# Expert stage of a mixture-of-experts kernel: expert numbers read once in eight steps, table places eight at a time, stores issued from other queues

## The reference

```
x = x + rwkv_block(layernorm(x))     # time mix: projections, a scan over 1024 tokens; channel mix
x = x + ffn(layernorm(x))
# ffn, over N = 8192 tokens:
gates = sigmoid(xt @ expert_sel.T)                 # 32 experts
sel_val, sel_idx = top_k(gates, 4)                 # 4 experts per token
scores = relu(einsum('nd,edf->nef', xt, keys))     # keys:   32 x 256 x 128
out = einsum('nef,efv->nv', scores * gate_full, values)   # values: 32 x 128 x 256
```

## Time and profile before

| | us |
|---|---|
| median of three runs | 1266.48 |
| the profiled execution's own time | 1261.35 |
| its span, first to last instruction | 1259.5 |
| PE / PEld busy | 1107.5 (88%) / 953.2 (76%) |
| DVE / ACT / POOL busy | 1015.1 (81%) / 752.8 (60%) / 760.8 (60%) |
| mean granted TensorE clock | 0.958 |

### The profile page before, as it was taken

One profiled execution on the slowest core, in us unless ns is written; L12 is line 12 of the kernel. 1 busy time (PEld: TensorE's weight loads), 2 busy tenths in 40 slices (PEclk: granted clock), 3 DMA queues, 4 the chain that ended last, 5 costly groups with the idle time before them and its releaser, 6 DMA issues.

```text
span 1259.5 us, 24103 instructions
## 1 busy us (share of the span) xinstructions
PE 1107.5 (88%) x6830; PEld 953.2 (76%) x6831; DVE 1015.1 (81%) x2268; ACT 752.8 (60%) x1504; POOL 760.8 (60%) x868
## 2 busy tenths in 40 slices
PE   6799999999999999999999997377799898799870
PEld 6678888788787887887787876377799898689860
DVE  3788899899899898899899885864478888678874
ACT  4467567567568567567568557444566566456550
POOL 2434377568558558668568666620077777657776
PEclk9799999999999999999999999589999999899995
DMA  9422134234224323324322128356599999899994
GB/s 342 153 85 101 39 130 141 85 110 142 96 96 146 108 79 137 102 94 145 102 87 80 65 75 350 129 181 204 160 307 348 356 356 350 292 310 360 346 315 126
DMA packets 131134, 227.55 MB, mean 181 GB/s; under 512 B 15584, under 2 KB 74976, under 8 KB 129632
## 3 DMA queue, kind: packets, MB, share of 16 engines
q1 hardware_dynamic: 82272, 121.49, 28.1%
q0 software_dynamic: 24576, 67.14, 16.1%
q10 hardware_dynamic: 24192, 37.76, 8.0%
HBM read 100.50 MB, written 125.83 MB: 180 GB/s over the span
## 4 chain that ended last, share of the span: by engine, by line
POOL 29%; PE 20%; issue 18%; DVE 13%; ACT 8%; DMA 7%; ACTq 3%; POOLq 1%; DVEq 0%; SPq 0%
POOL lists L1340 13%; PE ps L452 7%; POOL ye L1758 6%; DMA ye<-sorted_rows,place_of 5%; PE ps L1567 2%; POOL th_r L1383 2%; POOL rs L1294 2%; POOL xp L1370 2%; ACTq L1648 2%; DVE resid L1707 2%; PE ps L1584 2%; DVE xp L998 1%; ACT xt_hi L1666 1%; ACT y L1676 1%; DVE stats L880 1%
## 5 line engine op out<-in xcount | busy, mean ns | idle before, releaser
L1758 POOL DMA_INDIRECT ye<-sorted_rows,place_of x256 | 247.9, 968 | 176.6 <-DMA sorted_rows<-y 88.9
L1707 DVE SCALAR_TENSOR_TENSOR resid<-ye,gates,resid 128x256 f32<-128x256 f32 x256 | 123.1, 481 | 78.1 <-DMA ye<-sorted_rows,place_of 36.9
L1567 PE MATMUL ps<-keys,xt_hi 128*128 x576 | 149.7, 337 | 37.7 <-DVE xt_lo L1720 28.9
L1340 POOL DMA_INDIRECT lists<-rows_even,slot x128 | 142.8, 1115 | 46.0 <-issue 40.3
L1340 POOL DMA_INDIRECT lists<-rows_odd,slot x128 | 138.8, 1085 | 47.0 <-issue 40.3
L1663 ACT ACTIVATE sums<-ps 128x256 f32<-128x256 f32 x144 | 55.3, 384 | 170.9 <-PE ps L1609 122.7
L1567 PEld LDWEIGHTS ps<-keys,xt_hi 128*128 128x128 f32 x576 | 111.2, 193 | 48.8 <-issue 48.5
L1040 DVE TENSOR_TENSOR k_lo<-ksq,k_hi 128x512 fp32r<-128x512 f32 x128 | 117.5, 934 | 18.3 <-ACT k_hi L778 18.2
L1570 PE MATMUL ps<-keys,xt_lo 128*128 x576 | 129.9, 226 | 0.0
L769 ACT ACTIVATE kr<-ps,bias_k 128x512 f32<-128x512 f32 x128 | 86.7, 683 | 47.2 <-PE ps L452 44.5
L1570 PEld LDWEIGHTS ps<-keys,xt_lo 128*128 128x128 f32 x576 | 112.7, 196 | 0.0
(11 more groups left out here) (213 smaller groups left out, 3229.3 us busy)
## 6 DMA issues: line engine op xcount, KB each, us to landing
lists<-zeros SPq DMA_DIRECT2D x18, 2048.0 KB, 10.3
xr<-lists SPq DMA_DIRECT2D x120, 256.0 KB
sorted_rows<-y ACTq DMA_DIRECT2D x120, 256.0 KB
x_sb<-in_x SPq DMA_DIRECT2D x16, 512.0 KB, 4.4
residual<-xp SPq DMA_DIRECT2D x16, 512.0 KB, 5.1
experts_raw<-in_expert_in SPq DMA_DIRECT2D x8, 1024.0 KB, 15.1
resid<-residual SPq DMA_DIRECT2D x16, 512.0 KB, 7.4
out_dram<-resid SPq DMA_DIRECT2D x15, 512.0 KB, 6.5
```

The source lines that it names most:

```text
L1340: pool.indirect_dma_start(lists, bass.IndirectOffsetOnAxis(ap=slot[:, q, n:n + 1], axis=0), rows[q][:, n // TOPK, :], None).then_inc(last_ ...
L1567: pe.matmul(cols, xt_hi[:, home, c], keys[:, bass.ds(e, 1), k].rearrange("p a h w -> p (a h w)"), start=k == 0, stop=False, skip_group_che ...
L1707: dve.scalar_tensor_tensor(acc, ye[:, j, k, :], gate, acc, ALU.mult, ALU.add).then_inc(sum_step, 1)
L1758: pool.indirect_dma_start(ye[:, j, k, :], None, sorted_rows[0:(tile + 3) * OPENED * UNIT, :], bass.IndirectOffsetOnAxis(ap=place_of[:, n:n ...
```

## The change

TensorE's numbers are read by one function at every eighth step, for the keys and values of the steps up to the next read, and stay in registers. GpSimd, which has nothing to do while the head runs, issues the head's stores, and reads eight table places at a time; SP also reads eight places at a time. SP issues the stores of the other 120 batches, batch `i-12` behind the rows of batch `i`. ACT issues none. The head's stores have semaphores of their own (`y_head`). The body of the hardware loops is 24 steps instead of 48: 48 steps are written out as before, then the body runs four times.

```diff
+STORE_LAG = HOMES[0] + Y_LAG
...
-    SPAN = 6 * RING
+    SPAN = 3 * RING
...
-            table[0:1, first:first + FOLD], engines=(eng.engine,), min_val=0, max_val=last,
+            table[0:1, first:first + HELD * FOLD], engines=(eng.engine,), min_val=0, max_val=last,
...
+        def store(b, r):
+
+            q = r % YB
+            sp.wait_ge(ycopy_ready, b + 1)
+            sp.dma_start(sorted_rows[bass.ds(b * (FOLD * UNIT), FOLD * UNIT), :]
+                         .rearrange("(p f) d -> p f d", f=FOLD), y[:, q]).then_inc(y_stored[q], 16)
...
+            if within(i, HEAD_BATCHES + STORE_LAG, NSTEPS + STORE_LAG):
+                store(i - STORE_LAG, r - STORE_LAG)
...
-        def experts_of(b, r, use):
...
+        def read_experts(i, r):
+
+            first, end = r - (Y_LAG if r == 0 else H_LAG), r + RING - H_LAG
+            if isinstance(i, int):
+                first, end = max(first, r - i), min(end, r - i + NSTEPS)
+            if first >= end:
+                return
+            _, found = nc.values_load_multi_w_load_instructions(
+                plan_expert[0:1, bass.ds((i - r + first) * SUB, (end - first) * SUB)], engines=(pe.engine,),
...
-            experts = experts_of(b, q, "keys")
+            experts = held[q]
...
-            experts = experts_of(b, q, "values")
+            experts = held.pop(q)
...
         def step(i, r, pair):
+            if r % RING == 0:
+                read_experts(i, r)
...
     def on_scalar(act):
-        def store(b, r):
...
-            done = r - Y_LAG - 1
-            if done % WIDE == WIDE - 1 and within(i, Y_LAG + WIDE, NSTEPS + Y_LAG + 1):
-                store(BATCHES * pair + done // WIDE, done // WIDE)
...
-                if q % WIDE == 0:
-                    after(act, y_stored[home], landed(q // WIDE, pair, YB))
+                if isinstance(i, int) and i - Y_LAG - YB < HEAD_BATCHES:
+                    after(act, y_head[home], 16 * FOLD * ((i - Y_LAG) // YB))
+                else:
+                    act.wait_ge(y_stored[home], 16 * ((SPAN // YB) * pair + q // YB - HEAD_BATCHES // YB))
...
     def on_gpsimd(pool):
+        for b in range(HEAD_BATCHES):
+            if b % HELD == 0:
+                held = held_rows(pool, plan_store, b * FOLD, LIST_ROWS - FOLD * UNIT + FOLD - 1)
+            pool.wait_ge(ycopy_ready, b + 1)
+            for n, at in enumerate(held[b % HELD * FOLD:(b % HELD + 1) * FOLD]):
+                pool.dma_start(sorted_rows[bass.ds(at, UNIT, FOLD), :], y[:, b % YB, n, :]
+                               ).then_inc(y_head[b % YB], 16)
+        for stored in y_head:
+            pool.wait_ge(stored, 16 * FOLD * HEAD_BATCHES // YB)
```

More of the change, by code:

```diff
@@ L1427, in expert_phase @@
     rows_loaded, y_stored, ye_loaded = sems("rows_loaded", XB), sems("y_stored", YB), sems("ye_loaded", SUMMED)
+    y_head = sems("y_head", YB)
     resid_loaded, out_stored = sems("resid_loaded", RESIDS), sems("out_stored", RESIDS)
@@ L1435, in expert_phase @@
     SUM_END = SUM_LAG + 2 * NT * J
-    HELD = 4
-    PART_OF = P // FOLD
-    assert NSTEPS % SPAN == 0 and SPAN % HELD == 0 and SPAN // RING % RESIDS == 0 and HEAD_END <= SUB * SPAN
+    PART_OF, HELD = P // FOLD, 4
+    assert HEAD_BATCHES % HELD == 0
+    assert NSTEPS % SPAN == 0 and SPAN // RING % RESIDS == 0 and HEAD_END <= SUB * SPAN
     assert all(BATCHES % homes == 0 and HEAD_BATCHES % homes == 0 for homes in (XB, YB))
@@ L1473, in on_sync @@
     def on_sync(sp):
+        held = []
         def rows(b, r):
@@ L1477, in rows @@
             if in_head(b):
-                for n, at in enumerate(held_rows(sp, plan_row, b * FOLD, LIST_ROWS - UNIT)):
+                if b % HELD == 0:
+                    held[:] = held_rows(sp, plan_row, b * FOLD, LIST_ROWS - UNIT)
+                for n, at in enumerate(held[b % HELD * FOLD:(b % HELD + 1) * FOLD]):
                     sp.dma_start(xr[n * PART_OF:(n + 1) * PART_OF, q],
@@ L1514, in on_sync @@
         sp.wait_ge(scattered[1], 16 * (NT // 2 - 1) * J * TOPK)
-        for i in range(SPAN):
+        for i in range(2 * SPAN):
             if i == RING:
@@ L1522, in on_sync @@
                     load_resid(tile, tile, 0)
-        with sp.Fori(1, NSTEPS // SPAN) as pair:
+        with sp.Fori(2, NSTEPS // SPAN) as pair:
             for r in range(SPAN):
@@ L1538, in on_tensor @@
         held = {}
-        def experts_of(b, r, use):
[L1542 to L1551, removed]
+        def read_experts(i, r):
[6 more added lines that the diff above has]
+                plan_expert[0:1, bass.ds((i - r + first) * SUB, (end - first) * SUB)], engines=(pe.engine,),
+                min_val=0, max_val=E - 1,
+                skip_runtime_bounds_check_because="the plan writes all of the table, bounded, ahead of its "
+                                                  "semaphores")
+            for n in range(end - first):
+                held[first + n] = found[n * SUB:(n + 1) * SUB]
         def inner(i, r, pair):
             b, q = i - H_LAG, r - H_LAG
-            experts = experts_of(b, q, "keys")
+            experts = held[q]
             pe.wait_ge(x_ready, SPAN * pair + q // WIDE * WIDE + WIDE)
@@ L1641, in on_scalar @@
     def on_scalar(act):
-        def store(b, r):
[L1644 to L1652, removed]
-        def step(i, r, pair):
-            done = r - Y_LAG - 1
-            if done % WIDE == WIDE - 1 and within(i, Y_LAG + WIDE, NSTEPS + Y_LAG + 1):
-                store(BATCHES * pair + done // WIDE, done // WIDE)
-            if not within(i, 0, NSTEPS + Y_LAG):
-                return
+        def step(i, r, pair):
             act.wait_ge(pe_step, i + 1)
@@ L1681, in on_scalar @@
             act.wait_ge(stored, 16 * NT // 2)
-        for i in range(SPAN):
+        for i in range(2 * SPAN):
             step(i, i % SPAN, i // SPAN)
-        with act.Fori(1, NSTEPS // SPAN) as pair:
+        with act.Fori(2, NSTEPS // SPAN) as pair:
             for r in range(SPAN):
                 step(SPAN * pair + r, r, pair)
-        for i in range(NSTEPS, NSTEPS + Y_LAG + 1):
+        for i in range(NSTEPS, NSTEPS + Y_LAG):
             step(i, i % SPAN, i // SPAN)
@@ L1741, in on_vector @@
                 places_sorted(dve)
-        with dve.Fori(1, NSTEPS // SPAN) as pair:
+        with dve.Fori(2, NSTEPS // SPAN) as pair:
             for r in range(SPAN):
@@ L1752, in on_gpsimd @@
             for q in range(YB):
-                pool.wait_ge(y_stored[q], landed(batches + YB - 1 - q, 0, YB))
+                after(pool, y_stored[q], 16 * ((batches - HEAD_BATCHES) // YB))
             for j in range(J):
```

## The result

The changed kernel takes **1254.49 us** (median of 4 runs, 1253.58 to 1255.42) against 1266.09 us (median of 4 runs, 1264.07 to 1266.69) of the kernel before beside it. The ratio is 0.9905, with a 95% interval of 0.9883 to 0.9927: it is faster by some 12 us. Forecast were 1241.9 us, 24.6 us less than before; the time lies in the range of 1231 to 1260, but less than half of the forecast gain came.

The account below looks back on a forecast made before the run. POOL's gathers were taken as the bound: head's end, gathers, waits and tail make the span. It summed 899.7 + 247.9 + 76.5 + 4.7 + 6.1 = 1234.9, 24.6 less; from 1266.5 that gives 1241.9 us, range 1231 to 1260.

Parts of the forecast that it names:

- Edit 1: Head's stores go from ACT to GpSimd, priced at 2.50 us a batch: gathers begin at 899.7, 13.5 us sooner.
- rival 4: Head: a plain DMA of GpSimd is cheap and PE sets the pace, 1236 us or 1231; chance 0.15.
- Edit 2: Loop body of 24 steps: code stays in the sequencer's memory, branches cost 0.2 us each, covered; 11.1 us won.
- rival 1: PE's loop: the new body doesn't stay in the sequencer's memory, three branches stall, 1275 us, slower; chance 0.08.
- Edits 3 and 4: PE's reads once in eight steps and SP's 120 stores: set together at nothing, between -4.7 and +18 us.
- Rival 3: Stores land later from SP's queue, each tile waits 1.2 us longer: 1260 us; chance 0.10.
- PE has slack against POOL already: Steady part: PE needs 18.2 us for a tile's eight steps against POOL's 20.0, so fewer reads win little.

Follow-up runs that it names:

- x10: Kernel before with only the head's stores moved to GpSimd, which reads eight table places at a time: 1249.69 us, ratio 0.9864.
- x9: Kernel before with only the loop body cut to 24 steps: 1256.75 us, ratio 0.9922.
- x8: Changed kernel with ACT issuing the 120 stores and TensorE reading as before, two reads of eight numbers per four steps: 1235.22 us, ratio 0.9757.
- x1: Changed kernel with TensorE's reads as before, two of eight numbers per four steps; stores stay on SP: 1247.02 us, ratio 0.9848.
- x5: Changed kernel with SP's store put ahead of its load of rows in each step: 1237.77 us, ratio 0.9791.
- x2: Changed kernel with the 120 stores issued by ACT again; reads once in eight steps stay: 1244.87 us, ratio 0.9836.
- x6: Changed kernel with SP's store ahead of its rows and TensorE reading eight numbers every four steps: 1229.18 us, ratio 0.9731.
- x7: Changed kernel with the 120 stores issued by ACT and TensorE reading eight numbers every four steps: 1235.74 us, ratio 0.9780.
- the last three: x9, x10 and x11, run together on one chip: 1256.75, 1249.69 and 1231.25 us; the kernel before beside them had a median of 1265.48 us.
- x11: Changed kernel with SP's store ahead of its rows and TensorE reading four numbers every two steps: 1231.25 us, ratio 0.9730.
- x4: Changed kernel with TensorE reading eight numbers every four steps; stores stay on SP: 1247.21 us, ratio 0.9871.
- x3: Changed kernel with each TensorE read, once in eight steps, taking only two numbers, output not the reference's: 1248.34 us, ratio 0.9864.

## Why the prediction was wrong

**Edit 1, the head: right in kind, cheaper than priced.** Forecast −13.5 us, the first gather came 17.6 us sooner. A plain DMA of GpSimd lasts 0.539 us and a pair of them 1.13, where 2.50 were counted; the row taken, the indirect DMA, was near in engine and size but not in kind. What came is rival 4: PE sets the head's pace, POOL's pair waits 1.1 us for each copy, and the first gather at 895.7 stands near the 893.8 of that rival. Its landing took 4.1 us from the last store's issue, not 3.2. x10 alone shows −15.8 by medians.

**Edit 2, the body of 24 steps: right.** All five branches are short and the code queues fall silent behind the loop's first round (rival 1 is out). One detail in it and ahead of it was wrong: TensorE writes out 24 steps and runs its body five times, with four taken branches, while SP, ACT and VectorE write out 48 and run it four times. It changes nothing in the sum, since a branch costs 0.2 us. What was won by it is the least sharp of the terms: 8.7 us alone (x9), where 11.1 were forecast, 14.5 between x10 and x8, which also differ in SP's reads and of which 5.5 are x10's later first gather.

The Trainium skill (Runtime: NRT & Kernel Launch, section Instruction fetch mechanics) gives a memory of 128 KiB, by which the body stays, and a window of two pages, by which each taken branch would stall. The trace agrees with the first and not with the second: the five branches of the body of 480 matmuls last 0.08 to 0.21 us.

**Edits 3 and 4, "together at nothing": this step failed.** Together they cost 19.3 us (1254.5 against the 1235.2 of x8), just over the far end of 18 that was set for them. Both sentences under it were wrong.

- Of the reads the sum of their time was weighed (4 x 0.96 less 1.2), and one read of 16 or 24 numbers was taken to last 1.2 us. One of 16 lasts 2.93 in the median and one of 24 up to 4.49; the earlier trace rows showed only reads of 8 or fewer. And even the sum would have been the wrong measure: TensorE is idle for the part of each read that is longer than the work in its queue (at 1133 us that was 0.9 us, and 3.66 us idle), and behind that read TensorE ran for some 3 us at a clock of 0.51. "PE has slack against POOL already" no longer held: 18.0 us for eight steps became 21.9, against POOL's 20.0. The cost is 7 to 9 us.
- Of the stores it said that SP "gets to that step when VectorE has finished step `i-6`, in which ACT copied just this batch: so it doesn't wait long". VectorE's step ends late exactly at the end of a tile, where it waits for a gather of the tile's rows, and exactly there the store is the one for which POOL will wait. The copy doesn't wait for VectorE's whole step, the store did. In the changed kernel the delay is 0.77 us in the median and 3.53 at the most, in x1 up to 4.0. The cost is 12 us against stores from ACT (x1 to x8), 17 to 18 against the order of x5.

**Rival 3** had the size (1260 where it came out at 1254.5) and the sign that it named, waits for `sorted_rows<-y` at tile after tile. Its mechanism was another: company in the queue and a later landing. The landing is 0.3 us later in the median (7.5 us against 7.3 in x2, and 6.8 in x1, from SP again); what is late is the issue. The named bound, that the time from first gather to end be near 335 us, marked the forecast as wrong at once: it was 358.0, 22.8 more, of which 22.1 are POOL's waits (26.8 less 4.7).

**The sum, redone** with what the runs show: 1266.1 less 29.8 (edits 1 and 2, x8, with SP's reads) less 1.1 (that job's kernel before was 1265.0, not 1266.1) plus 19.3 is 1254.5. It closes because x8 and the changed kernel define its terms; what is independent is that the order of the queue and the reads, taken away one at a time, give 16.7 and 8.6 us, and that then POOL's waits are 1.0 us.

**A better version.** x6 takes 1229.2 us, 0.9731 of the kernel before (0.9696 to 0.9767), 25 us less than the changed one, with nothing but the order of two blocks and a shorter read. Its span of 1225.5 is 892.3 to the first gather, 248.4 busy, 77.8 of gaps, 1.0 of waits, and 6.0 behind it: what bounds it now is POOL's own pace and the head.

**Left open.** Why stores from ACT with short reads (x7, x8: 1235) stay 6 us behind stores from SP in the good order (x6: 1229). POOL waits 4 to 5 us longer there, and its gathers are 1.3 to 1.9 us longer busy; what delays the rows was not traced. By which path the swap wins what the delays don't account for. Also why the kernel before ran over 1259 to 1274 us beside the last three, where it kept within 3 us in its first runs: differences under some 5 us between kernels are not told from noise here, and the one of 6 us between x8 and x6 only just.

## What to carry to other kernels

When a DMA moves to another engine's queue, it takes over every wait that stands ahead of it there: write down what the instruction before it waits for, at the moment when the result is needed, not in the average step. Put what others wait for ahead of what only fills a distant buffer. Judge an instruction that blocks a sequencer by its single length against the work queued behind it, not by the sum over all of them; fewer and longer can be worse than more and shorter.

## What the runs showed of the hardware

- A plain DMA of 128 rows of 1 KB costs GpSimd 0.54 us to issue, an indirect one of the same bytes 0.95 and a gap of 0.30.
- A register read from a table in SBUF, with the DMA engines at a share of 0.95 to 0.98, took in the median 0.65 us for mostly 4 numbers (x11), 0.98 (x6) and 1.32 (x4) for mostly 8, and 2.93 for 16 (the changed kernel; 2.58 in x5), with 2.7, 3.2, 2.9 and 3.6 us at the most. Reads of 24 numbers took 2.53 to 4.49. A read of two numbers once in eight steps still took 1.56 (x3): the count is not all of it, and what else sets it was not found.
- A loop body of 480 matmuls branched in 0.2 us in every round, one of 960 stalled 5.7 and 6.4 us at its taken branch (x10, before).
- TensorE had been idle for 3.66 us and had run again for 1.5 us at the full clock when the granted clock fell to its lower level (0.51 from 1139 to 1142 us); it was 0.96 in the 5 us behind that.
- A gather that waited for a 256 KB store, with the DMA engines at a share of 0.95 to 0.98, began 5.5 to 8.4 us after the store's issue, from SP's queue and from ACT's alike (changed kernel, x1, x2, before).
